# Sending a window from another queue, packing two values an edge, and idle products in a sorting loop of a graph kernel

## What is computed

```
q = (embeds[rows] @ qW)   k = (embeds[cols] @ kW)   v = (embeds[cols] @ vW)     # rows = src, cols = dst
scores = clip(sum over a head of q * k, -10, 10);  exp_s = exp(scores)
w = exp_s / (segment_sum(exp_s, rows)[rows] + 1e-8)
res = segment_sum(w * v, rows);   out = layernorm(x + (x + res))
```

## Time and profile before

| | us |
|---|---|
| three runs | 1925.74, 1977.9, 1931.81 |
| their median | 1931.81 |
| the profiled execution, its own time | 1937.22 |
| its span, first to last instruction | 1935.2 |
| mean granted clock of TensorE | 0.893 of full |

### The profile page before, as it was taken

One profiled execution on the slowest core, in us unless ns is written; L12 is line 12 of the kernel. 1 busy time (PEld: TensorE's weight loads), 2 busy tenths in 40 slices (PEclk: granted clock), 3 DMA queues, 4 the chain that ended last, 5 costly groups with the idle time before them and its releaser, 6 DMA issues.

```text
span 1935.2 us, 56068 instructions
## 1 busy us (share of the span) xinstructions
PE 1572.6 (81%) x19964; PEld 1477.9 (76%) x19965; DVE 1438.2 (74%) x2978; ACT 1007.0 (52%) x1846; POOL 900.1 (47%) x764
## 2 busy tenths in 40 slices
PE   5936777777777787787767499999999999999991
PEld 4725666666666676676766499999999999999991
DVE  6887657666767575666664188888888888888887
ACT  4333434434544443444444366666666666666664
POOL 6223445555555554555555344444444444444441
PEclk8657879878989887888899699999999999999996
DMA  7565667776776676777677687777777777777741
GB/s 233 205 226 192 232 228 270 264 262 251 259 284 255 251 252 221 260 260 270 244 286 262 251 288 240 243 245 239 246 243 239 247 240 242 245 240 245 242 157 50
DMA packets 159452, 465.03 MB, mean 240 GB/s; under 512 B 36995, under 2 KB 59267, under 8 KB 152245
## 3 DMA queue, kind: packets, MB, share of 16 engines
q1 hardware_dynamic: 123572, 301.16, 47.1%
q0 software_dynamic: 35840, 163.36, 21.0%
HBM read 271.21 MB, written 209.73 MB: 249 GB/s over the span
## 4 chain that ended last, share of the span: by engine, by line
PE 61%; another core or an unknown queue 14%; DVE 11%; issue 6%; ACT 4%; SPq 2%; DMA 1%; DVEq 0%; POOL 0%; ACTq 0%; POOLq 0%
PE meta L1213 11%; PE sum_bank L1213 11%; PE two_b L1151 8%; PE two_a L1151 8%; PE two_a L1234 6%; PE two_b L1234 6%; ACT work L918 3%; PE one_d L1224 3%; PE one_c L1224 3%; DVE work L1486 2%; PE meta L1169 1%; PE one_d L1180 1%; DVE work L1493 1%; SPq L832 1%
## 5 line engine op out<-in xcount | busy, mean ns | idle before, releaser
L637 POOL DMA_INDIRECT sorted_rows<-work x448 | 486.2, 1085 | 474.5 <-issue 303.5
L700 POOL TENSOR_TENSOR work<-work 128x768 f32<-128x768 f32 x236 | 351.1, 1488 | 447.5 <-ACT work L955 447.5
L1151 PE MATMUL two_a<-work 128*128 128x192 bf16 x2688 | 308.2, 274 | 84.6 <-ACT work L918 68.3
L1151 PE MATMUL two_b<-work 128*128 128x192 bf16 x2688 | 307.5, 271 | 51.2 <-ACT work L918 41.8
L1151 PEld LDWEIGHTS two_a<-work 128*128 128x128 f16 x2688 | 251.0, 109 | 109.1 <-ACT work L918 53.9
L1151 PEld LDWEIGHTS two_b<-work 128*128 128x128 f16 x2688 | 255.0, 109 | 75.1 <-ACT work L918 48.8
L918 ACT ACTIVATE work<-two_a 128x768 f32<-128x768 f32 x224 | 181.0, 808 | 155.9 <-PE two_a L1151 94.6
L1493 DVE TENSOR_TENSOR work<-work,one_d 128x700 f16<-128x700 f16 x112 | 93.7, 877 | 207.8 <-remote 198.6
L918 ACT ACTIVATE work<-two_b 128x768 f32<-128x768 f32 x224 | 181.4, 810 | 128.2 <-PE two_b L1151 67.7
L964 ACT ACTIVATE work<-work 128x1024 f32<-128x1024 bf16 x236 | 247.2, 1047 | 0.0
L1213 PE MATMUL meta<-work 128*128 128x100 f32 x1888 | 235.9, 278 | 0.8 <-DVE acc L1564 0.8
(11 more groups left out here) (228 smaller groups left out, 2244.9 us busy)
## 6 DMA issues: line engine op xcount, KB each, us to landing
work<-sorted_rows SPq DMA_DIRECT2D x472, 392.0 KB, 3.5
work<-sorted_local SPq DMA_DIRECT2D x56, 1024.0 KB
sorted_rows<-pad_rows SPq DMA_DIRECT2D x49, 392.0 KB, 4.6
work<-kv_table SPq DMA_DIRECT2D x112, 144.0 KB
sorted_rows<-work POOLq DMA_INDIRECT x448
kv_table<-work SPq DMA_DIRECT2D x12, 576.0 KB, 3.4
work<-in_x SPq DMA_DIRECT2D x12, 192.0 KB, 4.3
sorted_local<-work SPq DMA_DIRECT2D x56, 8.0 KB
```

What stands on the lines that cost most here:

```text
L637: pool.indirect_dma_start(out=rows_dram, out_offset=bass.IndirectOffsetOnAxis(ap=place_now[:, p, u, b:b + 1], axis=0), in_=payload[:, p, u ...
L700: pool.tensor_tensor(now[:, :, 0:D].rearrange("p c (h f) -> p c h f", h=HEADS), blk[:, k, :, :, D:2 * D].rearrange("p m c (h f) -> p (m c) ...
L1151: mm = pe.matmul(to, picked[:, u % 2, k * P:(k + 1) * P], window[:, u, :, n, :], start=(n == 0), stop=(n == 2))
```

## The change

- The windows are issued by ACT's DMA queue instead of SP's. ACT loads the two window numbers from SBUF into registers at the start of its part of an iteration and issues window u right after its four copies of group u, with no wait on PE's signal of its own.
- The store of the turned offsets (`local_dram`) is issued by ACT as well, right after L933, with a wait on its own copy and one on `brow_in` of two iterations before. SP keeps only `brow`, with its waits.
- An edge carries two values instead of four: the tag, with what lies above ten bits of the target's offset packed above it, and the low ten bits of the offset. So `vals` takes two multiplications instead of four, a product of `sort` is 32 columns wide instead of 64, and ACT's copy of the values is 64 wide instead of 96. The branch `slow` gets more steps to take the values apart.
- In `kv(1)`, behind the products for the places and ahead of the wait for `picked` and the window, PE does 16 products of constants (`below_h` by `ident_h`, 128 columns) into unused PSUM.
- In the prologue, the per-edge parts are made with one step less, and the groups' bases are kept in float32 once.

```diff
-    NV = 4
-    TW = (NV - 1) * NCH
+    NV = 2
+    TW = NV * NCH
+    FILLERS = 16
...
 @block.sync, emit:
-                if c is not None and following:
-                    c1 = plus(sp, c, 1)
-                    los, at_c = bases(c1), counts(sp, c, G2, 1)
                 if b is not None:
-                    sp.wait_ge(local_rows_made, plus(sp, b, 1))
-                    sp.sem_inc(sp_turn, 1)
-                    sp.dma_start(local_dram[half]..., local_rows[0:QUAD * NCH, :]).then_inc(local_out, 16)
-                if c is not None and following:
-                    window_of(0, los[0], at_c)
-                if b is not None:
                     sp.wait_ge(local_out, times(sp, b, 16, 16))
...
-                if c is not None and following:
-                    for u in range(1, QUAD):
-                        window_of(u, los[u], at_c)
...
 @block.scalar, emit:
+                if following:
+                    los = words(act, base_regs, base_i, times(act, plus(act, c, 1), QUAD), N - 1)
...
                     act.activation(local_rows[0:QUAD * NCH, :], turned_v[0:QUAD * NCH], ACT.Copy).then_inc(local_rows_made, 1)
+                    if not (isinstance(b, int) and b < 2):
+                        act.wait_ge(brow_in, times(act, b, 16, -16))
+                    act.wait_ge(local_rows_made, b1)
+                    act.dma_start(local_dram[...], local_rows[0:QUAD * NCH, :]).then_inc(local_out, 16)
                 if c is not None:
-                    rows(0)
-                    rows(1)
+                    for u in range(QUAD):
+                        rows(u)
+                        if following:
+                            window_of(u, los[u])
...
 @block.tensor, kv(u):
                     mm.then_inc(dest_made[u % GSEM], 1)
+                    if u:
+                        for _ in range(FILLERS):
+                            pe.matmul(spare_ps, below_h[:], ident_h[:], start=True, stop=True)
                     group_done(pe, pick_made, u, done_c)
...
 @block.vector:
-                    for v, held in enumerate((src_tag, dst_hi, dst_lo, dst_local)):
+                    for v, held in enumerate((src_tag, dst_near)):
```

More of the change, by code:

```diff
@@ L157, in columns @@
             return cols_work[:, n, :].bitcast(F16).rearrange("p (g c) -> p g c", c=COLS)
-        src_tile, src_tag, dst_hi, dst_lo, dst_local, inner = (columns(n) for n in range(6))
+        src_tile, src_tag, dst_near, inner = (columns(n) for n in (0, 1, 2, 5))
         x_all = cols_work[:].rearrange("p a b -> p (a b)")[:, 0:NT * D].rearrange("p (t d) -> p t d", t=NT)
@@ L229, in gnn_program @@
         dst_part, at = share(at, [NCH], F32)
+        far_part, at = share(at, [NCH], F32)
+        tag_part, at = share(at, [NCH], F32)
+        base_part, at = share(at, [NCH], F32)
         place_now, dst_now = place_now.bitcast(U32), dst_now.bitcast(U32)
@@ new lines, in slow @@
+                    pool.tensor_scalar(far_part, far_part, ROUND, None, ALU.add).then_inc(slow_step, 1)
+                    pool.wait_ge(slow_step, made[4])
+                    pool.sem_inc(pool_turn, 1)
+                    pool.tensor_scalar(far_part, far_part, -ROUND, float(1 << SPREAD_BITS), ALU.add, ALU.mult
+                                       ).then_inc(slow_step, 1)
+                    pool.wait_ge(slow_step, made[5])
+                    pool.tensor_tensor(dst_part, dst_part, far_part, ALU.add).then_inc(slow_step, 1)
@@ new lines, in slow @@
+                    pool.wait_ge(slow_step, made[6])
+                    pool.tensor_tensor(dst_part, dst_part, base_part, ALU.add).then_inc(slow_step, 1)
+                    pool.wait_ge(slow_step, made[7])
+                    pool.sem_inc(pool_turn, 1)
+                    pool.tensor_copy(dst_now, dst_part).then_inc(slow_step, 1)
+                    pool.tensor_scalar(far_part, far_part, -(2.0 ** (TAG_BITS - SPREAD_BITS)), None, ALU.mult
+                                       ).then_inc(slow_step, 1)
@@ L666, in slow @@
+                    pool.wait_ge(slow_step, made[9])
+                    pool.tensor_tensor(payload[:, p, u, :, TAG], far_part, tag_part, ALU.add).then_inc(slow_step, 1)
+                    pool.wait_ge(slow_step, made[10])
                     pool.sem_inc(pool_turn, 1)
@@ L904, in _, with window_of @@
             act.activation(q3[0:NREST, FULL_NT], last3[0:NREST, 2], ACT.Copy).then_inc(q_kept, 1)
-            def emit(a, b, c, p=None):
+            base_regs = [act.alloc_register(f"base{u}") for u in range(QUAD)]
+            act.wait_ge(tables_made, 1)
+            for n in range(2):
+                act.wait_ge(table_out[n], 16 * (TI // 2))
+            act.wait_ge(rest_out, 32)
+            def window_of(u, lo):
+                act.dma_start(window[:, u].rearrange("p x a b -> p (x a b)"), kv3[bass.ds(lo, P), :]
+                              ).then_inc(window_in[u], 16)
+            def emit(a, b, c, p=None):
+                following = c is not None and not (isinstance(c, int) and c + 1 >= NQ)
+                if c is None and b == 1:
+                    los = words(act, base_regs, base_i, 0, N - 1)
+                    for u in range(QUAD):
+                        window_of(u, los[u])
+                if following:
+                    los = words(act, base_regs, base_i, times(act, plus(act, c, 1), QUAD), N - 1)
                 if c is not None:
@@ L933, in emit @@
                     act.activation(local_rows[0:QUAD * NCH, :], turned_v[0:QUAD * NCH], ACT.Copy).then_inc(local_rows_made, 1)
+                    if not (isinstance(b, int) and b < 2):
+                        act.wait_ge(brow_in, times(act, b, 16, -16))
+                    act.wait_ge(local_rows_made, b1)
+                    act.dma_start(local_dram[bass.ds(low_bits(act, b, 1), 1)].rearrange("o r p -> (o r) p"),
+                                  local_rows[0:QUAD * NCH, :]).then_inc(local_out, 16)
                 if c is not None:
-                    rows(0)
-                    rows(1)
+                    for u in range(QUAD):
+                        rows(u)
+                        if following:
+                            window_of(u, los[u])
             first_phase(act, emit)
```

54 lines of the change are left out of this document (24 added, 30 removed).

## The result

The changed kernel takes 2034.2 us in the median of four runs (2030.48 to 2048.13), the kernel before 1942.9 in the same comparison: a ratio of 1.049, interval 1.044 to 1.055. The ratio is taken from runs in the chip's faster state alone, so it isn't the quotient of the two medians (1.047). Forecast were 1945 and a range from 1875 to 2005.

A forecast was written before the change was run, and what follows sets the result against it. Bound: the first phase's chain of eight scatters, late signal and missing copies. The profiled 1937.2 us plus 14.5 for ScalarE's issues, others 0, gave 1951.7, lying 5.4 above the median: 1946, said as 1945; range 1875 to 2005.

The forecast's parts named there:

- The bound: First phase: eight scatters (10.5 to 11.5 us), late signal (about 1 us), missing copies (2 to 5 us); 16.63 us an interval.
- passed: Iteration with two or more copies of the next group before the last scatter's end; 17 of 55, averaging 14.6 us.
- held: Iteration in which TensorE's results reach the others late while GpSimd issues scatters; the other 38 intervals, averaging 17.5 us.
- 29 x 0.5 = 14.5 us: ScalarE's store between L933 and the copies, on the path where the late signal releases L933; bounds 9 and 26, or 0.
- The slower rival: Passed iterations become held: over 1970 if more than eight of 17, 1986 with 14, 2006 with all; chance 0.30.
- The faster rival: `brow`'s traffic beside the first scatters holds the signals; moved ahead, 1887 with 20 more passed, 1835 with all 38; chance 0.27.
- The sentence against it in the prediction: The passed and the held iteration of the rows have `brow` at the same place before their scatters.
- The windows on ScalarE: Window 0 hidden ahead of group 1's tag and copies; window 1 ahead of L926, followed by turning that waits for counts anyway.
- The 16 products: TensorE, ahead of group 1's picks: 0.96 to 1.53 us, taken as 1.0; cost 0 on the scatters.
- The clock rival: The 16 products keep TensorE's clock at its upper level of 2.4 GHz: 15 us back, so 1930; chance 0.05.
- Two values: Two of four VectorE multiplications go: gain 0, at most 0.65 us an iteration (36 us in all).
- no late window: Windows queued behind `brow` might arrive late, TensorE waiting for a transfer: named as another way to be wrong, no size given.

The follow-up runs named there:

- h1: Kernel before with one idle GpSimd multiplication of 512 elements, and a wait for it, between the scatters of the two groups: 1900.4 us, ratio 0.961.
- f4: Kernel before with ScalarE's copy of the turned offsets done in eight pieces, no DMA moved: ratio 1.0269.
- f1: Kernel before with only the store issued by ScalarE, behind its four copies of group 0: ratio 1.0047.
- r_after: The changed kernel again, unchanged, where the kernel before took 1952 us: 2034.5 us, ratio 1.042.
- g3: The changed kernel once more, unchanged, run beside one with 32 products: ratio 1.0411 to the kernel before.
- f3: The changed kernel without its 16 products, with late signals: ratio 1.0333 to the kernel before.
- f2: Kernel before with windows and store on ScalarE's queue, four values, no products, with late signals: ratio 1.0353.
- g2: Kernel before with SyncE issuing `brow` right behind the store, nothing else changed: ratio 1.0083.
- e5: Kernel before with windows on ScalarE's queue; SyncE keeps the store and issues `brow` right behind it: 1968.9 us, ratio 1.009.
- e3: Kernel before with windows and store on ScalarE's queue, four values, no products, with prompt signals: ratio 1.0159.
- e4: The changed kernel without its 16 products, with prompt signals: ratio 1.0175 to the kernel before.
- e6: Kernel before with only the store of the offsets on ScalarE's queue, ahead of the copies: 2011.2 us, ratio 1.030.
- e1: Kernel before with two values an edge instead of four, all else as before, with prompt signals: ratio 0.9985.
- e2: Kernel before with the 16 products alone, four values, SP's queue as before, with prompt signals: ratio 1.0012.

## Why the prediction was wrong

- **The bound** (a chain of scatters, late signal and missing copies, with passed and held iterations) was right: in h1 no iteration is held, and its first phase is 38.6 us shorter, though GpSimd does more.
- **The step that failed** is "29 x 0.5 = 14.5 us", ScalarE's DMA issues: a delay counted once for each iteration in which it stands on the path, with the number of passed iterations kept at 17. The price for one was low but within its bounds: from the offsets' copy to the payload copy the median of the 40 iterations is 1.18 against 0.40 us, 0.78 us more, where I took 0.5, from 0.3 to 0.9. In the iteration shown ScalarE's idle time around the store is 0.71 us (658.36 to 659.07): the issue is 0.34 as assumed, 0.08 lie between the copy's end and it, and 0.29 behind it, which I had too low. It applied 40 times instead of 29, so all of it is 31 us of the 104. The larger error is the kind. In this loop a delay also changes how many iterations pass: 3 instead of 17, 41 us, for which the forecast had nothing. A copy that is 0.37 us longer was enough for 2.7% (f4), and the same store behind the copies costs 0.5% (f1). The last 31 us, held iterations that became longer by more than the delay, have no measured cause.
- **The slower rival** ("passed ones become held") named the mechanism and gave it 0.30; it should have been the forecast. Its signs came true: over 40 waits (43) and intervals over 17.5 (18.5). It predicted "with 14" 1986 and with all 2006. That 14 fewer pass is luck of one execution; in r_after and g3 one iteration passes. The time was 2034 because the 52 held ones lengthened by 1.2 us each, where I had laid 0.5 on 29 of them. Its other reason, that shorter VectorE work lets GpSimd issue faster, isn't supported: two values alone are 0.9985 where signals are prompt, and f3 equals f2 within their intervals.
- **The faster rival** (`brow` holds the signals) is refuted by g2. The sentence against it in the prediction was the better evidence.
- **The windows on ScalarE** and the early `brow` were costed at nothing: e5 shows 0.9% for both together, and g2 0.8% for `brow` ahead of the window alone. Whether the window issues, which stand ahead of ScalarE's sorting copy, cost anything with late signals isn't shown.
- **The 16 products**: 1.05 us in 46 of 56 iterations of after, up to 1.87 in the others (I took 1.0, with 0.96 to 1.53). No run shows them to cost more than about 1%, and 16 more gain 1.3%.
- **The clock rival**: with 16 products the clock of the span fell, 0.893 to 0.869. In the iteration shown it is low behind the long gap that the hold leaves in TensorE's work. It gets to 0.90 with 32 products, and to 0.91 (300 to 1050 us) in h1, which adds none.
- **Two values, prologue, no late window, `brow` 1.5 to 3 us behind the store** (1.5 to 3.0, median 1.7): right, though in e3 and e4, with prompt signals, windows do come late. The first scatter came 2.1 us earlier, a little outside -1 to +1.

## What to carry to other kernels

Where an engine's signals get through only at certain moments, don't price a delay by its length alone: count how many iterations miss the moment, and put the forecast where small delays lead, not at their sum. A store of what the issuing engine has just written costs that engine more than the issue (0.71 us of idle time with an issue of 0.34 in the iteration shown); put it behind the work that others wait for (f1 against e6: 0.5 against 3.0%). A count that rests on a threshold moves when the change itself moves iterations across it; look at what the counted ones have in common before calling them a new kind. And a bound that shows as "remote" under a row of back-to-back scatters is worth one cheap test, a pause between them.

## What the runs showed of the hardware that I had not expected

- While GpSimd issues scatters back to back with 0.3 us between them, results of TensorE reach VectorE and ScalarE late, by 6.0 us in the iteration shown (650.49 to 656.51). Single ones come through between scatters, as at 644.11, and in h1 all come through in the pause of about 2 us, 0.7 us after the scatter ahead of it has ended. Back-to-back scatters alone don't do it: in e1 and e2 they follow each other in the same way, and nothing is late. What holds them isn't shown; `brow`'s traffic isn't it. Fewer or narrower scatters weren't tried.
- The same program took 1695 us in one session and 1943 to 2015 (medians) in the others; in the first, e1 and e2 have no held iteration and an interval of 12.2 us. It isn't tied to the chip's number in the records: the first session and that of f1 name the same one, with 1695 and 1947 us. What differs is open, and with it what the pause of h1 costs where signals are prompt; that wasn't tried. Nor was the pause in the changed kernel.
